# Graph attention on one core: a small projection in four column groups, later sums, other places for loads and sums, and a last row that ends on VectorE

## The reference

```
h = relu(layernorm(x))                      # [8192, 256]
g = inlayer2 @ W.T + b                      # [8192, 128]
f1 = g @ w1 + b1 ; f2 = g @ w2 + b2         # [8192] each
logits = f1[:, None] + f2[None, :]          # [8192, 8192]
coefs = softmax(leaky_relu(logits, 0.01) - 1e9 * (adj == 0), axis=-1)
out = x + coefs @ h                         # adj: [8192, 8192] int32
```

## Time and profile before

| | us |
|---|---|
| median of 3 runs | 1448.58 (1448.45 to 1448.86) |
| the profiled execution | 1447.21 |
| its span, first to last instruction | 1445.4 |
| TensorE busy | 1408.1 (97%) |
| VectorE busy | 1279.7 (89%) |
| ScalarE busy | 612.4 (42%) |
| GpSimd busy | 267.6 (19%) |

### The profile page before, as it was taken

The page is one execution under the profiler, slowest core; times in us unless marked ns, Lnnn a source line. Parts: engine busy times, 40 slices in busy tenths (PEclk is TensorE's granted clock), DMA queues, the critical chain, the costliest instruction groups (busy, mean ns, idle before and its releaser), DMA issues.

```text
span 1445.4 us, 33386 instructions
## 1 busy us (share of the span) xinstructions
PE 1408.1 (97%) x12623; PEld 1246.3 (86%) x12623; DVE 1279.7 (89%) x1313; ACT 612.4 (42%) x714; POOL 267.6 (19%) x269
## 2 busy tenths in 40 slices
PE   8489999999999999999999999999999999999998
PEld 7377888888888888888888888888888888888887
DVE  5899999989899898989989898998989989898994
ACT  2895344344444343444434344343434434344430
POOL 0582111101111110111111011111101111110111
PEclk9789999999999999999999999999999999999999
DMA  9978999999999999999999999999999999999940
GB/s 301 310 181 181 234 230 230 231 232 220 208 211 215 209 211 209 215 209 210 215 209 210 207 216 211 209 215 209 210 207 217 209 211 215 207 212 207 215 103 8
DMA packets 110168, 302.43 MB, mean 209 GB/s; under 512 B 11716, under 2 KB 44612, under 8 KB 110148
## 3 DMA queue, kind: packets, MB, share of 16 engines
q1 hardware_dynamic: 100144, 289.58, 89.4%
q10 hardware_dynamic: 10004, 12.59, 2.9%
HBM read 293.73 MB, written 8.39 MB: 209 GB/s over the span
## 4 chain that ended last, share of the span: by engine, by line
PE 94%; ACT 2%; DVE 2%; DMA 1%; issue 1%; ACTq 0%; POOL 0%; SPq 0%; POOLq 0%; DVEq 0%
PE acc L1024 61%; PE acc L1026 30%; PE rp L979 2%; DMA adj_sb<-in_adj_dram 1%; DVE wgt L824 1%; ACT h_f L570 1%; DVE wT L834 0%; ACT H L576 0%; PE rp L993 0%; ACT o_room L584 0%; DMA w<-in_L_gnn_w_dram 0%; PE small L966 0%; ACT rp L554 0%; DVE b_word L810 0%; ACT mask L554 0%
## 5 line engine op out<-in xcount | busy, mean ns | idle before, releaser
L1024 PE MATMUL acc<-H,wT 128*128 128x257 f16 x8192 | 1356.2, 273 | 9.7 <-DVE wT L834 6.9
L1026 PE MATMUL acc<-H,wT 128*128 128x257 f16 x4096 | 1120.0, 273 | 0.0
L1024 PEld LDWEIGHTS acc<-H,wT 128*128 128x128 bf16 x8192 | 802.1, 98 | 113.0 <-DVE wT L834 6.9
L554 ACT ACTIVATE mask<-adj_sb 128x1024 bf16<-128x1024 int32 x504 | 519.2, 1053 | 542.8 <-DVE wgt L824 428.8
L834 DVE STREAM_TRANSPOSE wT<-wgt 128x1024 f32<-128x1024 f32 x512 | 634.0, 1239 | 129.2 <-PE acc L1026 129.1
L824 DVE SCALAR_TENSOR_TENSOR wgt<-b_word,c_word,mask 128x1024 f32<-128x1024 f32 x504 | 626.9, 1256 | 0.0
L1026 PEld LDWEIGHTS acc<-H,wT 128*128 128x128 f16 x4096 | 401.5, 98 | 50.5
L474 POOL TENSOR_TENSOR x_res<-o_room,x_res 128x256 f32<-128x256 f32 x64 | 66.5, 1039 | 1115.2 <-ACT o_room L561 1069.5
L561 ACT ACTIVATE o_room<-acc,r_den 128x256 f32<-128x256 f32 x64 | 30.2, 471 | 251.0 <-DVE r_den L853 251.0
L479 POOL TENSOR_TENSOR o_room<-o_room,x_res 128x256 f32<-128x256 f32 x64 | 82.3, 1287 | 5.3
L476 POOL TENSOR_SCALAR o_room<-h_mean,no_nb 128x256 f32<-128x256 f32 x64 | 60.8, 950 | 0.0
(11 more groups left out here) (91 smaller groups left out, 173.2 us busy)
## 6 DMA issues: line engine op xcount, KB each, us to landing
adj_sb<-in_adj_dram SPq DMA_DIRECT2D x504, 512.0 KB, 8.6
x_res<-in_x_dram SPq DMA_DIRECT2D x64, 128.0 KB, 4.0
out_dram<-o_room SPq DMA_DIRECT2D x64, 128.0 KB, 4.2
H<-in_x_dram ACTq DMA_DIRECT2D x16, 256.0 KB, 12.2
H<-in_x_dram SPq DMA_DIRECT2D x16, 256.0 KB, 12.7
adj_sb<-in_adj_dram ACTq DMA_DIRECT2D x8, 512.0 KB, 13.1
wgt<-in_L_gnn_inlayer_dram ACTq DMA_DIRECT2D x8, 256.0 KB, 9.0
wgt<-in_L_gnn_inlayer_dram SPq DMA_DIRECT2D x8, 256.0 KB, 9.6
```

Of the source, the lines that this page charges most:

```text
L554: nc.scalar.activation(place, adj_sb[:, c, g * CQ:(g + 1) * CQ], ACT.Relu, scale=M_SCALE).then_inc(m_ready, 1)
L1024: pe.matmul(acc[:, par, 0:DV], w_hi[:, slot, t, :], H[:, j, part, 0:DV], start=(j == 0 and part == 0), stop=False)
L1026: mm = pe.matmul(acc[:, par, 0:DV], w_lo[:, slot, t, :], H[:, j, 0, 0:DV], start=False, stop=(j == ROWS - 1))
```

## The change

1. **f in four column groups.** V has 32 stationary columns instead of 128. The matmuls m = 2g and 2g + 1 write PSUM rows 32g to 32g + 31, so that four groups hold four partial sums. `f_of_strip` issues e = 0 for the four groups, then e = 1. The sum over groups is made later: f2_of picks it up in the matmuls of `b_exponents`, and new matmuls `f_sums(c)` with the stationary matrix `same` add the transposed parts. `chunk_f` is split into `chunk_turn` and `chunk_max`. `keep_busy(n)` issues n matmuls of 128 columns on ones into a room of PSUM that is not in use.
2. **x issues.** ScalarE issues each of its x strips one place earlier in its program, except 6 and 7, which move behind the first masks; the second f copy goes ahead of `sums(1)`.
3. **Values' sum.** h_sum, its matmul and the h_mean copy move from the end of row 1 into strips 0, 1 and 5 of row 2.
4. **Last row.** ScalarE's scaling and GpSimd's three steps become two VectorE operations; the store is split over SyncE and ScalarE.
5. **Order.** The parts of rows 0 and 1 are reordered on all engines.

```diff
-        V = h_f32[:, 1, :, :].rearrange("p t d -> p (t d)").rearrange(
-            "p (m i) -> p m i", m=FM)
+        V = h_f32[:, 1, 0, :].rearrange("p (m i) -> p m i", m=FM)
...
+            def keep_busy(n):
+                for _ in range(n):
+                    pe.matmul(acc[:, 0, 0:P], ones[:, :], ones[:, :], start=True, stop=True)
+
             def f_of_strip(k):
 
                 pe.wait_ge(in2T_ready, 2 * (k + 1))
-                for m in range(FM):
-                    mm = pe.matmul(rp[:, k // SC, SQ * (k % SC):SQ * (k % SC + 1)], V[:, m, :], in2T[:, k % 2, m, :],
-                                   start=(m == 0), stop=(m == FM - 1))
+                for e in range(2):
+                    for g in range(Q):
+                        m = 2 * g + e
+                        mm = pe.matmul(rp[B * g:B * (g + 1), k // SC, SQ * (k % SC):SQ * (k % SC + 1)], V[:, m, :],
+                                       in2T[:, k % 2, m, :], start=(e == 0), stop=(e == 1))
                 mm.then_inc(f_done, 1)
+
+            def f_sums(c):
+
+                pe.wait_ge(f_cols_ready, c + 1)
+                pe.wait_ge(pick_ready, Q + 1)
+                parts = f_cols[:, c * CQ:(c + 1) * CQ].rearrange("p (j a o v) -> p a j o v", a=Q, o=2, v=Q)
+                for a in range(Q):
+                    mm = pe.matmul(f_sum_ps[B * a:B * (a + 1), c * ROWS:(c + 1) * ROWS], same[:, :],
+                                   parts[:, a, :, :, 0], start=True, stop=True)
+                mm.then_inc(f_sum_ps_ready, 1)
...
-            for k in range(NS):
-                f_of_strip(k)
+            f_of_strip(0)
+            keep_busy(4)
...
             b_exponents(0)
-
+            f_sums(0)
+            f_of_strip(5)
+            keep_busy(4)
...
+            load_x(act, 1, 2, (2, 3))
             sums(0)
-            load_x(act, 1, 2, (2, 3))
+            load_x(act, 2, 3, (2, 3))
             f_to_sbuf(0)
...
             load_x(act, 4, 5, (2, 3))
+            f_to_sbuf(1)
             sums(1)
-            f_to_sbuf(1)
             load_x(act, 5, 6, (2, 3))
             squares(1)
-            load_x(act, 6, 7, (2, 3))
-            load_x(act, 7, 8, (2, 3))
             act.wait_ge(f2_rel_ready, 1)
...
-            for n in range(10):
+            for n in range(14):
                 pe.matmul(small[:, 0, 0:P], ones[:, :], ones[:, :], start=True, stop=True)
...
             finish_2(0, 0, 0)
-            dve.wait_ge(h_sum_done, 1)
-            nc.vector.tensor_scalar(h_sum[:, :], hs_ps, 1.0 / (H_SCALE * N), None, ALU.mult).then_inc(h_sum_ready, 1)
-            weights(2, 2, 0)
             weights(2, 3, 0)
...
-                    if is_row(I, 2) and u == 2:
+                    if is_row(I, 2) and u == 0:
+                        dve.wait_ge(h_sum_done, 1)
+                        nc.vector.tensor_scalar(h_sum[:, :], hs_ps, 1.0 / (H_SCALE * N), None,
+                                                ALU.mult).then_inc(h_sum_ready, 1)
+                    if is_row(I, 2) and u == 5:
                         dve.wait_ge(h_mean_ps_ready, 1)
                         nc.vector.tensor_copy(h_mean[:, :], hm_ps).then_inc(h_mean_done, 1)
...
+            nc.vector.scalar_tensor_tensor(out=x_res[:, 1, :], in0=acc[:, 1, 0:D], scalar=r_den[:, 1:2],
+                                           in1=x_res[:, 1, :], op0=ALU.mult, op1=ALU.add).then_inc(last_sum, 1)
+            dve.wait_ge(last_sum, 1)
+            nc.vector.scalar_tensor_tensor(out=o_sb[:, 1, :], in0=h_mean[:, :], scalar=no_nb[:, 1:2],
+                                           in1=x_res[:, 1, :], op0=ALU.mult, op1=ALU.add).then_inc(last_ready, 1)
```

More of the change, by code:

```diff
@@ L139, in graph_attention @@
         F_ps = small[:, 1, 384:385]
+        f_sum_ps = small[:, 0, 256:256 + 2 * ROWS]
         hs_ps = small[:, 1, 0:D]
@@ L661, in _ @@
             mask_part(1, 1, 1)
+            values(12)
             mask_part(1, 2, 1)
-            values(12)
             high_of_values(12)
@@ L687, in _ @@
             row_tiles(act, body, ahead=1)
-            for i in range(2):
-                scale_rows(ROWS - 2 + i, i, ROWS // 2 - 1)
+            scale_rows(ROWS - 2, 0, ROWS // 2 - 1)
+            act.wait_ge(last_ready, 1)
+            act.dma_start(out_rows[ROWS - 1][P // 2:P], o_sb[P // 2:P, 1, :]).then_inc(last_stored, 16)
         @block.vector
@@ L774, in variance @@
                                         ALU.add).then_inc(var_ready, 1)
-            for k in range(2, NS):
-                turn_in2(k)
-            chunk_f(0)
+            turn_in2(2)
+            turn_in2(3)
+            turn_in2(4)
+            turn_in2(5)
+            chunk_turn(0)
+            turn_in2(6)
+            turn_in2(7)
+            chunk_max(0)
+            chunk_turn(1)
             raw_stats(16, 20)
-            chunk_f(1)
+            chunk_max(1)
             raw_stats(20, 24)
@@ L1069, in _ @@
             products(1, 1, 7)
-            pe.wait_ge(h_sum_ready, 1)
-            pe.matmul(hm_ps, ones[:, :], h_sum[:, :], start=True, stop=True).then_inc(h_mean_ps_ready, 1)
             pe.wait_ge(scaled, 1)
@@ L1080, in body @@
                     products(I, par, k)
+                    if is_row(I, 2) and k == 1:
+                        pe.wait_ge(h_sum_ready, 1)
+                        pe.matmul(hm_ps, ones[:, :], h_sum[:, :], start=True,
+                                  stop=True).then_inc(h_mean_ps_ready, 1)
             row_tiles(pe, body, ahead=1)
```

146 lines of the change are left out of this document (90 added, 56 removed).

## The result

The changed kernel takes 1456.13 us in the median of 20 runs (1444.13 to 1459.49), the kernel before 1448.80 (20 runs, 1447.55 to 1449.56): ratio over all runs 1.0039, interval 1.0028 to 1.0051 (of the medians alone 1.0051). It is slower by 0.4%, where 0.6% faster was forecast, and it has become unsteady: five runs lie between 1444.1 and 1450.2, fifteen between 1454.2 and 1459.5, while the 20 runs before lie within 2 us. The profiled execution is one of the fifteen (1455.49 us, span 1453.4, against 1447.21 and 1445.4 before).

What follows compares the result with a forecast made beforehand. TensorE's steady stream was taken as the bound from 132.58 us, with ScalarE, then VectorE, limiting before it. 5.9 us ahead plus 2.2 at the tail gave 8.1 less: 1439.1 profiled, 1440.5 us timed, range 1437.0 to 1444.8.

Steps and rivals of the forecast that it cites:

- No stall, and nothing to spare: Strip 5 of row 3: possible at 158.4 despite the later h_mean copy, exactly when TensorE reaches it.
- the store order stalls row 3: Rival: h_mean copy or load 2 us later stops TensorE 2 us at strip 5 of row 3; 1442.5 us, chance 0.15.
- Front, 2.2 us: Work up to the exponentials: column groups and moved x issues start them at 48.6 instead of 50.80, 2.2 us gained.
- f32 groups do not overlap: Rival: f's column-group matmuls take 0.44 us each, so exponentials start near 60.4; 1452.3 us, chance 0.06.
- x strips 6 and 7 "cost nothing": Loads moved behind the first masks: VectorE reads them at about 66, after their bytes are through at 55; 0 us.
- Reordering, 1.9 us: Rows 0 and 1: two long VectorE low parts blocked by GpSimd instead of three, 1.9 us gained.
- 11 us for waits: TensorE before strip 1 of row 2: could finish its work at 115.3, leaving 11 us, so VectorE decides.
- h_sum wait, 2.3 less 0.5: Values' sum moved into row 2: VectorE's 2.30 us wait goes, the mean's matmul between strips costs 0.5.
- Tail, 2.2: Last row after the last matmul: two VectorE operations save 2.2 us, the halved store changes nothing.

Runs made afterwards that it cites:

- e2: Kernel before with only the h_mean copy moved from strip 2 to strip 5 of row 2; 1455.18 us, ratio 1.0040.
- e10: Changed kernel with the fillers of e5 and, on ScalarE, the sums of strip 1 ahead of the second f copy; 1452.01 us, ratio 1.0024.
- e1: Changed kernel with the mean's matmul behind strip 0 of row 2 and the h_mean copy back at strip 2; 1445.86 us, ratio 0.9991.
- e5: Changed kernel with 22 and 11 filler matmuls instead of 4 and 4 behind strips 3 and 4 of f; 1452.37 us, ratio 1.0026.
- e12: e11 with f as before the change: whole-width matmuls, no column groups, no fillers between strips; 1443.92 us, ratio 0.9965 to the kernel before.
- e7: Changed kernel with ScalarE's scaling of row 2 ahead of the masks of row 4's second half, mean still late; 1449.44 us, ratio 1.0004.
- e9: Changed kernel with two VectorE statistics swapped, so that it asks for x strip 7 last; 1450.39 us, ratio 1.0010.
- e11: Changed kernel with the edits of e1, e9, e5 and e10 at once; 1444.92 us, ratio 0.9976.
- e13: Changed kernel with the statistics' order of e9 and the fillers of e5, mean still late; 1448.27 us, ratio 1.0001.
- e8: Changed kernel with mean early as in e1, x strips 6 and 7 issued as in e3, and the fillers of e5; 1446.93 us, ratio 0.9990.
- e4: Kernel before with only the last row ended on two VectorE operations and its store split; 1447.25 us, ratio 0.9990.
- e3: Changed kernel with the issues of x strips 6 and 7 on ScalarE back right behind the squares; 1451.26 us, ratio 1.0020.

## Why the prediction was wrong, step by step

Forecast and profiled execution are 16.4 us apart (1439.1 and 1455.49). 8.3 of them are there when strip 1 of row 2 starts (134.50 against 126.2), 6.7 are the stop in row 3 and the slow clock behind it, 0.7 the tail.

**"No stall, and nothing to spare"** is the step that failed. The path was right as far as it went: h_mean, row 0's store, SyncE's queue, the load of row 4. Two things were wrong in it. It was followed to strip 5 of row 3 through the masks of the first half; but ScalarE has masks of row 4's second half ahead of the scaling of row 2, and the last strip of row 3 waits for that scaling. That end of the path has less room than strip 5: in the kernel before, the scaling ran at 165.62 and was needed at 169.5, 3.9 us, where strip 5 had 6.7 (157.6 against 164.3). With the prediction's own figures, a copy 0.9 us later and all else 5.9 us earlier, it gives a stop of 2.9 us. And its start was taken from a front 6.4 us early: the copy came at 143.83, not 135.7. e2 prices the step alone at 6.4 us, more than the 2 us of the rival "the store order stalls row 3", which had the mechanism at strip 5 but not the 2.7 us at 1.2 GHz that follow the stop. The wait is not always the same: 0.7 to 4.3 us with the mean late. After one of 1.8 us in row 3 the window's clock stayed at 1.00 (e10), after those of 2.7 and more there it fell; yet after 2.91 us of idle time up to 109.44 in e1 it stayed at 1.00, so the length of a stop alone does not tell.

**Front, 2.2 us.** The size of the column groups was nearly right (0.13 us a matmul, 0.11 taken), so the rival "f32 groups do not overlap" fell. f ended at 41.5 instead of 39.5: behind the pause before strip 4 (4.98 us) TensorE ran at 1.2 GHz, the strip in 1.93 us and the exponents in 2.88, and strips 5 to 7 wait behind these. That is 1.1 of the 2.0 us (f ends at 40.4 in e5); most of the rest is that a strip with its fillers takes 2.09 us at the full clock, not 1.8. The prediction named the slow clock, up to 1.8 us, and left it out of the sum. Held at 2.4 GHz (e5) the exponentials start at 49.59, and with the sums ahead of the copy (e10) at 48.84. The forecast's 48.6 can be had. But e12 has 48.38 with f as it was: the gain is that of the x issues moved away from ahead of the exponentials on ScalarE, which the prediction also counted, and TensorE's share in it is nothing. VectorE's chain of the maximum ends last there, 0.6 us later than the 47.7 it was given (f_rel at 48.09, 0.26 us).

**x strips 6 and 7 "cost nothing"** was wrong. VectorE asks for strip 7 at 68.1, not far from the 66 taken, but two of its four parts are issued only at 53.95 and 54.4, beside SyncE's adj, and the slowest of these landings took 16.7 us after the change, 16.3 in e5, 19.1 in e7, but 13.6 in e1 and 13.5 in e9. Four profiles (after, e5, e7, e10) show waits of 2.96, 3.21, 5.47 and 3.18 us, e1, with the same order, none. Between after and e1, the same program up to S, lie 0.9 us at the exponentials, 3.0 of this wait and 1.3 behind it, 5.2 in all. The sum of the transferred bytes, on which the step rested, says nothing on which bytes come first.

**Reordering, 1.9 us.** By the trace of after nothing was won: three long low parts, and the weights at 107.83 lose 1.8 us besides. With VectorE on time (e1, e9, e11, e12, e13) one is left, of 2.2 us: eight low parts cost 1.1 us more than eight short ones instead of 5.4 (four of 1.43 us and four of 1.21 in e11 by their means, against 1.18). So the count of the sequence was even too high for a VectorE that is on time, and VectorE 3.9 us later (at 71.09 instead of 67.17), in the same program, has three. Two things of the sum were wrong besides. The weights lose 1.8 us in every profile with the new order; and the third long low part before (112.17) lay behind the last turned strip that TensorE waited for (110.06) and ahead of VectorE's idle 2.30 us for h_sum, so there was nothing to win from it. After the change the long one from 80.53 ends 1.07 us after GpSimd's from 80.55, as in the kernel before (1.08). The Trainium skill (SBUF — State Buffer, "SBUF: two separate sides") has the two engines share a port pair, locked for an instruction. The traces agree to 0.01 us between these two. By e1 and after, the cost hangs on when the engines arrive and not on the order of the program alone. S moved much less than this (123.4 to 125.5 in these five against 124.25 to 125.7 in three profiles of the order of before). TensorE, which was given "11 us for waits", had 8.6 us of them from 72.2 to 109.4 in e1 and then none until S: from there on it decides, not VectorE.

**h_sum wait, 2.3 less 0.5** was right: span less S falls by 2.0 beyond the tail in e1, e8, e11 and e12 alike. **Tail, 2.2**: 1.5 by e4 and by the trace. The operations give 2.0 (1.0 us from 1449.64 where it was 3.0 from 1440.17), the split store takes some 0.5 back, which was counted as nothing.

**What stays open.** Where VectorE asks for strip 7 in the order of the change, its landing explains much of the spread: after, e1 and e7 are one program up to S, and S follows the landing. Not explained is why e9, where strip 7 is asked for last, still has a range of 9.8 us, and e13, with the fillers besides, one of 7.5. Nor is it shown why the other ranges are smaller: 2.7 where f is whole (e12, five runs), 5.0 and 3.5 where x is issued early (e3, e8), 5.1, 3.1 and 5.1 with the fillers (e5, e10, e11), 1.6 to 2.2 in the kernels with the order of before (e2, with the late mean, 4.7). Other loads landing a few us apart, those of adj for instance, would do it, but each kernel has a trace of one execution only.

## What to carry to other kernels

Follow a moved instruction to everything that stands behind its waiters in *program order*, not only to what needs its data: here a small copy reached TensorE through GpSimd, a store queue, a load, four masks and a scaling that needed none of them. Where engines block each other, a stretch has no cost of its own but one that depends on when it starts; price a late load there with the blocking it brings back, and look at the range of the runs as well as their median. And before an engine's work is made faster, ask who reads it last: f on a quarter of TensorE's time was worth nothing, and the kernel with f at full width (e12) has the lowest median and, of all with the new order of rows 0 and 1, the smallest range.
